# Gated mixing written as one stream over the eight batches, with one of its operations on ScalarE

## The chip, the core and the metric

The kernel runs on one core of a Trainium2 chip. Its engines work side by side, each through its own list of instructions: TensorE (PE in the rows; PEld is its weight load), VectorE (DVE), ScalarE (ACT), GpSimd (POOL) and SyncE (SP), which issues transfers here. They wait for one another at semaphores only. TensorE writes to PSUM, eight banks of 512 f32 values on each of 128 partitions; VectorE and ScalarE read from there. The metric is the device time of one execution in microseconds.

## What is computed

Eight sublayers run one after another on eight batches of 256 tokens with 256 features. Each is `x = layernorm(x + f(x))`. The change touches the fifth, the gated mixing:

```python
x = _layernorm(x + _L1_ffn_ref(...), axis=-1)
x = _layernorm(x + _L2_attn_ref(x, Wu, bu, Wv, bv, Wg1, bg1, Wg2, bg2, conv_w, conv_b), axis=-1)
x = _layernorm(x + _L2_ffn_ref(...), axis=-1)

def _L2_attn_ref(x, Wu, bu, Wv, bv, Wg1, bg1, Wg2, bg2, conv_w, conv_b):
    R, DH = 256, D // 4
    t = conv(x, conv_w)                  # one filter of three taps for each feature, along the tokens
    t_out = t + conv_b
    u = x @ Wu.T + bu
    v = x @ Wv.T + bv
    h = relu(x @ Wg1.T + bg1)            # 64 wide
    gates = sigmoid(h @ Wg2.T + bg2)
    u_gated, v_gated = u * gates, v * gates
    k_cumsum = cumsum(u_gated, axis=1)   # along the tokens
    return t_out + (k_cumsum * v_gated) @ Wu
```

## The kernel before

Everything is f32. The activations stay on the chip from the first sublayer to the last: `x_sb` holds tokens on the partitions, 16 tiles of 128 tokens, and `xT` holds the same with features on the partitions. Ahead of each stage `boundary` finishes the layer norm, turns `x_sb` by TensorE transposes (L161) and copies the result to `xT` (L169); all engines meet at a barrier on both sides of it. The stage of the gated mixing is `l2_mixing`.

For one batch (`T` = 256 tokens) TensorE has two pieces of work. The front is three groups: `g1`, the product of 64 rows (L1618), `u` and `v` (L1623, four products of 256 columns each), and `g2`, the gates (L1628), which needs `hT`, the relu that ScalarE makes of the first product (L1647). The back (L1635, L1637) adds the product of `go` with `Wu` and a product of `tc` with the unit matrix, which turns the convolution, in one PSUM bank.

ScalarE makes the relu and the sigmoid `ga` (L1650). VectorE does the rest of a batch in three pieces. The convolution `tc` is a centre tap with the bias (L1666, one instruction for each half of the features), the tap before (L1669) and the tap after (L1672). The mixing is `ug` and `vg` out of PSUM (L1677, L1678), the cumulative sum `cum` (L1681) and the product `go` (L1683). The output adds the finished bank to `x_sb` (L113) and measures mean and variance for the layer norm (L120, L124, L126).

The order is written by hand, as a hardware loop of four turns of two batches. In a turn TensorE does front, front, back, back. VectorE does convolution and mixing of the first batch, the same of the second, and then both outputs. All eight PSUM banks are in use, two of each kind, one for each batch of a turn: `HY` takes the product of 64 rows first and the stage's output later, `U`, `V`, and `GG` for the gates. So the first product of the next turn waits until VectorE has added the output out of the same bank (semaphore `z_ready`). `mix_ready` counts finished `go`, `y_ps` finished backs, `ga_ready` finished gates.

Of the kernel before, what the change touches and what calls it, by code (L numbers as in the profile page):

```python
# [8 lines left out]
P = 128  # L9
# [34 lines left out]
def ln_scratch(sb, n):  # L44
    return {"stats": sb("ln_stats", [P, n, 6]), "mv": sb("ln_mv", [P, n, 2]), "carrier": sb("ln_carrier", [P, 1])}
# [49 lines left out]
LN_STEPS = 2  # L95
# [1481 lines left out]
def l2_mixing(nc, c, x_sb, mv, xT, w, psum):  # L1577

    R, DH = 256, 64
    with ExitStack() as ctx:  # L1580
        sb = lambda name, shape, dt=F32: ctx.enter_context(nc.sbuf_tensor("l2a_" + name, shape, dt))
        sem = lambda name: ctx.enter_context(nc.semaphore("l2a_" + name))
        hT = sb("hT", [DH, 2, T])
        ga = sb("ga", [P, 2, 2, T])
        ug = sb("ug", [P, 2, 2, T])
        vg = sb("vg", [P, 2, 2, T])
        cum = sb("cum", [P, 2, 2, T])
        go = sb("go", [P, 2, 2, T])
# [8 lines left out]
        h_ready = sem("h_ready")  # L1597
        uv_ps = sem("uv_ps")
        g_ps = sem("g_ps")
        ga_ready = sem("ga_ready")  # L1600
        mix_ready = sem("mix_ready")
        y_ps = sem("y_ps")
        z_ready = sem("z_ready")
        steps = sem("steps")

        with nc.Block() as block:
            @block.tensor
            def _(pe):
                mm = nc.tensor.matmul
                w["early"](pe)  # L1610
                w["late"](pe)
                pe.sem_inc(z_ready, 2)
                with pe.Fori(0, B // 2) as b:
                    for i in range(2):
                        x = lambda k: xT[:, k, bass.ds(b * 2 * T + i * T, T)]
                        pe.wait_ge(z_ready, 2 * b + i + 1)
                        for k in range(KD):
                            last = mm(HY[i][0:DH, 0:T], w["g1"][:, k, :], x(k), start=(k == 0), stop=(k == KD - 1))  # L1618
                        last.then_inc(h_ps, 1)
                        for name, bk in (("u", U), ("v", V)):  # L1620
                            for m in range(2):
                                for k in range(KD):
                                    last = mm(bk[i][:, m * T:(m + 1) * T], w[name][:, k, m * P:(m + 1) * P], x(k),  # L1623
                                              start=(k == 0), stop=(k == KD - 1))
                        last.then_inc(uv_ps, 1)
                        pe.wait_ge(h_ready, 2 * b + i + 1)
                        for m in range(2):
                            last = mm(GG[i][:, m * T:(m + 1) * T], w["g2"][0:DH, m * P:(m + 1) * P], hT[:, i, :], start=True, stop=True)  # L1628
                        last.then_inc(g_ps, 1)
                    for i in range(2):  # L1630
                        pe.wait_ge(mix_ready, 2 * b + i + 1)
                        for t in range(TT):
                            y = HY[i][:, t * D:(t + 1) * D]
                            for k in range(2):
                                mm(y, go[:, i, k, t * P:(t + 1) * P], w["u"][:, k, :], start=(k == 0), stop=False)  # L1635
                            for k in range(KD):
                                last = mm(y[:, k * P:(k + 1) * P], tc[:, i, k, t * P:(t + 1) * P], c["id"], start=False, stop=(k == KD - 1))  # L1637
                        last.then_inc(y_ps, 1)

            @block.scalar  # L1640
            def _(act):
                nc.scalar.preload_act_table(ACT.Sigmoid)
                w["late"](act)
                with act.Fori(0, B // 2) as b:
                    for i in range(2):
                        act.wait_ge(h_ps, 2 * b + i + 1)
                        nc.scalar.activation(hT[:, i, :], HY[i][0:DH, 0:T], ACT.Relu, bias=w["bg1"][0:DH, :]).then_inc(h_ready, 1)  # L1647
                        act.wait_ge(g_ps, 2 * b + i + 1)
                        for m in range(2):
                            last = nc.scalar.activation(ga[:, i, m, :], GG[i][:, m * T:(m + 1) * T], ACT.Sigmoid, bias=w["bg2"][:, m:m + 1])  # L1650
                        last.then_inc(ga_ready, 1)

            @block.vector
            def _(dve):
                st = Steps(dve, steps, L2A_STEPS)
                nc.vector.memset(ones[:, :], 1.0)
                w["early"](dve)
                w["late"](dve)
                with dve.Fori(0, B // 2) as b:
                    st.begin(b)  # L1660
                    for i in range(2):

                        dve.wait_ge(h_ps, 2 * b + i + 1)
                        x = lambda k, at, n: xT[:, k, bass.ds(b * 2 * T + i * T + at, n)]
                        for k in range(KD):
                            last = nc.vector.tensor_scalar(tc[:, i, k, :], x(k, 0, T), w["conv"][:, k, 1:2], w["convb"][:, k:k + 1], ALU.mult, ALU.add)  # L1666
                        st.do(last)
                        for k in range(KD):
                            last = nc.vector.scalar_tensor_tensor(tc[:, i, k, 1:T], x(k, 0, T - 1), w["conv"][:, k, 0:1], tc[:, i, k, 1:T], ALU.mult, ALU.add)  # L1669
                        st.do(last)  # L1670
                        for k in range(KD):
                            last = nc.vector.scalar_tensor_tensor(tc[:, i, k, 0:T - 1], x(k, 1, T - 1), w["conv"][:, k, 2:3], tc[:, i, k, 0:T - 1], ALU.mult, ALU.add)  # L1672
                        st.do(last)
                        dve.wait_ge(uv_ps, 2 * b + i + 1)
                        dve.wait_ge(ga_ready, 2 * b + i + 1)
                        for m in range(2):
                            nc.vector.scalar_tensor_tensor(ug[:, i, m, :], U[i][:, m * T:(m + 1) * T], w["bu"][:, m:m + 1], ga[:, i, m, :], ALU.add, ALU.mult)  # L1677
                            last = nc.vector.scalar_tensor_tensor(vg[:, i, m, :], V[i][:, m * T:(m + 1) * T], w["bv"][:, m:m + 1], ga[:, i, m, :], ALU.add, ALU.mult)  # L1678
                        st.do(last)
                        for m in range(2):  # L1680
                            last = nc.vector.tensor_tensor_scan(cum[:, i, m, :], ones[:, :], ug[:, i, m, :], 0.0, ALU.mult, ALU.add)  # L1681
                        st.do(last)
                        nc.vector.tensor_tensor(go[:, i, :, :], cum[:, i, :, :], vg[:, i, :, :], ALU.mult).then_inc(mix_ready, 1)  # L1683
                    for i in range(2):
                        dve.wait_ge(y_ps, 2 * b + i + 1)
                        add_and_measure(nc, st, x_sb, mv, b * 2 * TT + i * TT, TT, two(HY[i]), lw, z_ready, 2 * b + i + 3)
                    st.end()


L2A_STEPS = 2 * (5 + LN_STEPS)  # L1690

def l2_ffn(nc, c, x_sb, mv, xT, w, psum):
# [1344 lines left out]
```

## Time and profile before

| | |
|---|---|
| time, median of 3 runs | 2721.08 us (2719.87 to 2721.51) |
| profiled execution: its own time, and the span from first to last instruction | 2712.49 us, 2710.7 us |
| TensorE, VectorE and ScalarE busy, share of the span | 87%, 69%, 51% |
| mean granted TensorE clock over the span | 0.943 |
| the gated mixing, first product to last statistics | 1510.25 to 1594.32 us, 84.07 us |
| the next stage, first transposes | 1597.75 us |

A row of the timeline begins with the start in microseconds from the span's start, and the length. The brackets at its end give the idle time of the engine before it and what ended that. An f32 product of the program shows as two records of TensorE, so `x4` is two products of the program. The granted clock is 1.00 at 2.4 GHz and 0.50 at 1.2 GHz, TensorE's two levels.

### The profile page before, as it was taken

Reading aid. Unit: us, or ns where it says so; the run is one execution under the profiler, and the core shown is the slowest. Engines: PE = TensorE matmul, PEld = TensorE weight load, DVE = VectorE, ACT = ScalarE, POOL = GpSimd, SP = SyncE. Lnnn points to the kernel's source line nnn. Section 1 sums busy time; section 2 is a strip of 40 time slices with the busy share of each in tenths; the row PEclk is TensorE's granted clock in tenths of the full one; section 3 lists DMA queues with packets and bytes.
Section 4 is the critical chain, followed back from the end, with each engine's and each line's share of the span. In section 5 each row is a group of like instructions: output and inputs, shape, how many; then the busy total and the mean of one; then the engine's idle time right before and its main releaser. Section 6 shows DMA issues by size and latency. Waiting matters only on the chain. (4 is left out here: it accounts for less than half of the span.)

```text
span 2710.7 us, 41350 instructions
## 1 busy us (share of the span) xinstructions
PE 2367.8 (87%) x13696; PEld 1866.6 (69%) x13696; DVE 1880.1 (69%) x4340; ACT 1373.0 (51%) x3717; POOL 456.8 (17%) x449
## 2 busy tenths in 40 slices
PE   7997999969999999999899779967777865999998
PEld 5665567657777778777777657755555544888887
DVE  3665488966655766575666668957777775888887
ACT  4665488864544544454521123338888773333332
POOL 2442200020000000000000000027777780000000
PEclk9999999989999999999999989979898876999999
DMA  4001077731001100110322000010000004222221
GB/s 150 12 8 67 3 160 147 155 72 36 23 11 35 35 19 15 35 35 18 121 63 63 0 0 0 1 53 9 5 4 4 8 1 159 63 64 72 72 63 59
DMA packets 67406, 130.21 MB, mean 48 GB/s; under 512 B 9944, under 2 KB 23256, under 8 KB 65880
## 3 DMA queue, kind: packets, MB, share of 16 engines
q1 hardware_dynamic: 67296, 128.81, 16.7%
q8 instruction: 61, 1.00, 0.1%
q14 instruction: 49, 0.40, 0.1%
HBM read 119.54 MB, written 2.69 MB: 45 GB/s over the span
## 5 line engine op out<-in xcount | busy, mean ns | idle before, releaser
L2180 POOL TENSOR_TENSOR l3a_pr<-l3a_pr,w_l3a_mask 128x1024 f32<-128x1024 f32 x32 | 75.6, 2361 | 1201.1 <-ACT l3a_pr L2247 1201.1
L2247 ACT ACTIVATE l3a_pr<-psum,l3a_nm 128x128 f32<-128x128 f32 (+1 forms) x512 | 207.4, 430 | 72.9 <-DVE l3a_nm L2355 72.9
L1135 ACT ACTIVATE l1a_pr<-psum,l1a_nb,l1a_rq 128x128 f32<-128x128 f32 (+1 forms) x256 | 127.3, 510 | 77.9 <-DVE l1a_nb L1221 74.1
L2355 DVE TENSOR_REDUCE l3a_nm<-psum 128x2 f32<-128x256 f32 (+1 forms) x256 | 124.8, 550 | 54.7 <-PE psum L2059 54.4
L2647 ACT ACTIVATE l3f_sg<-psum 128x512 f32<-128x512 f32 x96 | 57.5, 599 | 192.5 <-PE psum L2599 192.5
L2597 PE MATMUL psum<-l3f_x_hi,l3f_w_hi 128*128 128x512 f32 x384 | 151.8, 395 | 1.7 <-DVE l3f_w_lo L2683 1.7
L2598 PE MATMUL psum<-l3f_x_lo,l3f_w_hi 128*128 128x512 f32 x384 | 151.5, 395 | 0.0
L2599 PE MATMUL psum<-l3f_x_hi,l3f_w_lo 128*128 128x512 f32 x384 | 150.3, 392 | 0.0
L113 DVE TENSOR_TENSOR x_sb<-psum,x_sb 128x512 f32 (+2 forms) x44 | 36.6, 833 | 142.9 <-PE psum L1074 104.9
L372 POOL TENSOR_TENSOR l0a_pr<-l0a_pr,l0a_rec 128x256 f32<-128x256 f32 (+1 forms) x128 | 101.9, 828 | 142.3 <-DVE l0a_rec L462 142.3
L2631 ACT ACTIVATE l3f_w_hi<-w_l3f_all 128x768 fp32r<-128x768 f32 x96 | 81.4, 849 | 80.8 <-PE psum L2616 79.8
L2267 ACT ACTIVATE l3a_pr<-l3a_pr,l3a_nb,l3a_rec 128x128 f32<-128x128 f32 (+1 forms) x256 | 120.4, 570 | 3.3 <-POOL l3a_nb L2202 3.3
L1037 PE MATMUL psum<-l1a_kT,l1a_qT 128*128 128x128 f32 (+1 forms) x512 | 98.8, 337 | 22.7 <-ACT l1a_pr L1135 15.7
L1074 PE MATMUL psum<-l1a_kT,l1a_ko 128*128 128x256 f32 x512 | 112.6, 381 | 6.1 <-ACT l1a_ko L1124 6.1
L2193 POOL TENSOR_TENSOR l3a_pr<-l3a_pr 128x768 f32<-128x768 f32 x64 | 115.9, 1811 | 5.0
L1074 PEld LDWEIGHTS psum<-l1a_kT,l1a_ko 128*128 128x128 f32 x512 | 96.6, 190 | 20.4 <-issue 7.6
L2614 PE MATMUL psum<-l3f_w_hi,l3f_h_hi 128*128 128x256 f32 x384 | 108.9, 284 | 2.0 <-DVE l3f_h_lo L2733 1.9
L2247 ACT ACTIVATION_READ_ACCUMULATOR l3a_pr<-psum,l3a_nm 128x1 f32 x512 | 110.6, 216 | 0.0
L392 ACT ACTIVATE l0a_pr<-psum,l0a_nm 128x128 f32<-128x128 f32 (+1 forms) x256 | 103.6, 437 | 10.6 <-DVE l0a_nm L449 10.2
L2616 PE MATMUL psum<-l3f_w_hi,l3f_h_lo 128*128 128x256 f32 x384 | 108.7, 283 | 0.0
L2615 PE MATMUL psum<-l3f_w_lo,l3f_h_hi 128*128 128x256 f32 x384 | 108.6, 283 | 0.0
L838 DVE TENSOR_TENSOR l0f_act_h<-l0f_act_h,l0f_cbuf 128x512 f32<-128x512 f32 x128 | 88.2, 689 | 26.8 <-ACT l0f_act_h L728 14.3
(439 smaller groups left out, 6976.4 us busy)
## 6 DMA issues: line engine op xcount, KB each, us to landing
l0f_cbuf<-l0f_c_rows SPq DMA_DIRECT2D x128, 256.0 KB, 4.8
l1a_kT<-l1a_o_dram SPq DMA_DIRECT2D x64, 256.0 KB, 2.8
l3f_cbuf<-l3f_c_rows SPq DMA_DIRECT2D x64, 192.0 KB, 2.8
w_l3f_all<-l3f_all_dram SPq DMA_DIRECT2D x1, 9216.0 KB, 25.6
w_l1f_all<-l1f_c_rows SPq DMA_DIRECT2D x32, 256.0 KB, 3.2
l3f_cbuf<-l3f_c_rows SPq DMA_DIRECT2D x64, 128.0 KB, 2.9
w_l0f_w<-l0f_w_dram SPq DMA_DIRECT2D x2, 2048.0 KB, 10.1
l3f_cbuf<-l3f_c_rows SPq DMA_DIRECT2D x64, 64.0 KB, 2.6
```

The costliest lines, as they stand in the source:

```text
L1074: last = mm(PT[0][:, t * D:(t + 1) * D], oT[:, h, t * P:(t + 1) * P], wo[:, h, :], start=(h == 0), stop=(h == H - 1))
L1135: last = nc.scalar.activation(pr[:, n % 2, i, s], S[n % 2][:, i, s], ACT.Exp, bias=nb[:, n % 2, t, i:i + 1], scale=rq[:, t, 2 * n + i:2 * ...
L2193: nc.gpsimd.tensor_tensor(pr[:, r, 0, heads, :], pr[:, r, 0, heads, :], pr[:, r, 1, heads, :], ALU.add).then_inc(dif_ready, 1)
L2247: last = nc.scalar.activation(pr[:, r, a, g, k], S[:, g, k], ACT.Exp, bias=nm[:, i % 2, g, t:t + 1], accum_out=sums[:, r, a, g, t:t + 1])
L2267: last = nc.scalar.activation(pr[:, r, 1, g, k], pr[:, r, 0, g, k], ACT.Exp, bias=nb2[:, r, g, t:t + 1], scale=rec[:, r, 0, g, t:t + 1])
L2355: last = nc.vector.tensor_reduce(nm[:, i % 2, 2 * pair:2 * pair + 2, t], S[:, 2 * pair:2 * pair + 2, t * P:t * P + (t + 1) * P], AX.X, ALU ...
L2597: mm(bk[n % 2], hi, x_hi[:, k, chunk], start=(k == 0), stop=False)
L2598: mm(bk[n % 2], hi, x_lo[:, k, chunk], start=False, stop=False)
L2599: last = mm(bk[n % 2], lo, x_hi[:, k, chunk], start=False, stop=(k == KD - 1))
L2614: mm(Y[b % 2][:, t, :], h_hi[:, n % 2, tokens], hi, start=False, stop=False)
L2615: mm(Y[b % 2][:, t, :], h_hi[:, n % 2, tokens], lo, start=False, stop=False)
L2616: last = mm(Y[b % 2][:, t, :], h_lo[:, n % 2, tokens], hi, start=False, stop=(e == NH - 1 and t % 2 == 1))
```

## The change

The loop is gone: the eight batches are written out one after another on each engine. The work on TensorE is split into `front(n)` and `back(n)`, and their order is front(0), front(1), back(0), front(2), back(1), and so on to front(7), back(6), back(7). VectorE does convolution and mixing of batch n and then the output of batch n - 1. The product of 64 rows moves from the output's bank to the gates' bank `GG`, where the gates overwrite it after the relu; the output has its two banks to itself. ScalarE makes the centre tap with the bias (`Identity` with a scale and a bias of one value for each partition), ahead of the batch that needs it, and VectorE adds the outer two taps onto that after a wait for the new semaphore `tc_ready`. The semaphore waits follow: the first product waits for the gates of two batches earlier to be read, `u` and `v` for `mix_ready` of two batches earlier, the back for `mix_ready` and for the addition of two batches earlier, the sigmoid for `mix_ready` and the centre tap for `y_ps`, both of two batches earlier.

```diff
-        HY, U, V, GG = [bank(0), bank(1)], [bank(2), bank(3)], [bank(4), bank(5)], [bank(6), bank(7)]
+        Y, U, V, GG = [bank(0), bank(1)], [bank(2), bank(3)], [bank(4), bank(5)], [bank(6), bank(7)]
...
+                def front(n):
+                    i, tokens = n % 2, slice(n * T, (n + 1) * T)
+                    if n >= 2:
+                        pe.wait_ge(ga_ready, n - 1)
+                    for k in range(KD):
+                        last = mm(GG[i][0:DH, 0:T], w["g1"][:, k, :], xT[:, k, tokens], start=(k == 0), stop=(k == KD - 1))
+                    last.then_inc(h_ps, 1)
+                    if n >= 2:
+                        pe.wait_ge(mix_ready, n - 1)
...
+                    pe.wait_ge(h_ready, n + 1)
+                    for m in range(2):
+                        last = mm(GG[i][:, m * T:(m + 1) * T], w["g2"][0:DH, m * P:(m + 1) * P], hT[:, i, :], start=True, stop=True)
+                    last.then_inc(g_ps, 1)
+
+                def back(n):
+                    i = n % 2
+                    pe.wait_ge(mix_ready, n + 1)
+                    if n >= 2:
+                        pe.wait_ge(z_ready, n - 1)
...
-                pe.sem_inc(z_ready, 2)
-                with pe.Fori(0, B // 2) as b:
-                    for i in range(2):
-                        x = lambda k: xT[:, k, bass.ds(b * 2 * T + i * T, T)]
-                        pe.wait_ge(z_ready, 2 * b + i + 1)
...
+                front(0)
+                for n in range(B):
+                    if n + 1 < B:
+                        front(n + 1)
+                    back(n)
...
+                def centre(n):
+                    if n >= 2:
+                        act.wait_ge(y_ps, n - 1)
+                    for k in range(KD):
+                        last = nc.scalar.activation(tc[:, n % 2, k, :], xT[:, k, n * T:(n + 1) * T], ACT.Identity,
+                                                    bias=w["convb"][:, k:k + 1], scale=w["conv"][:, k, 1:2])
+                    last.then_inc(tc_ready, 1)
...
+                centre(0)
+                for n in range(B):
+                    i = n % 2
+                    act.wait_ge(h_ps, n + 1)
...
+                    act.wait_ge(g_ps, n + 1)
+                    if n >= 2:
+                        act.wait_ge(mix_ready, n - 1)
...
+                    if n + 1 < B:
+                        centre(n + 1)
...
+                def convolve(n):
+                    i = n % 2
+                    dve.wait_ge(tc_ready, n + 1)
...
+                for n in range(B):
+                    convolve(n)
+                    mix(n)
+                    if n >= 1:
+                        output(n - 1)
+                output(B - 1)
```

The operations themselves, their shapes and their number stay the same on TensorE. On TensorE, before, in one turn of the loop, this stands from the second batch's `u` on: its front, the back of the first batch, and the back of the second.

```order
L1623 MATMUL psum<-xT,w_l2a_u 128x256 x4
L1623 MATMUL psum<-xT,w_l2a_v 128x256 x4
L1628 MATMUL psum<-l2a_hT,w_l2a_g2 128x256 x2
L1635 MATMUL psum<-w_l2a_u,l2a_go 128x256 x2
L1637 MATMUL psum<-cf_sb,l2a_tc 128x128 x2
L1635 MATMUL psum<-w_l2a_u,l2a_go 128x256 x2
L1637 MATMUL psum<-cf_sb,l2a_tc 128x128 x2
L1635 MATMUL psum<-w_l2a_u,l2a_go 128x256 x2
L1637 MATMUL psum<-cf_sb,l2a_tc 128x128 x2
```

Now, from the `u` of batch 1 on: its front, the back of batch 0, and then the front of batch 2.

```order
L1624 MATMUL psum<-xT,w_l2a_u 128x256 x4
L1624 MATMUL psum<-xT,w_l2a_v 128x256 x4
L1629 MATMUL psum<-l2a_hT,w_l2a_g2 128x256 x2
L1640 MATMUL psum<-w_l2a_u,l2a_go 128x256 x2
L1642 MATMUL psum<-cf_sb,l2a_tc 128x128 x2
L1640 MATMUL psum<-w_l2a_u,l2a_go 128x256 x2
L1642 MATMUL psum<-cf_sb,l2a_tc 128x128 x2
L1617 MATMUL psum<-xT,w_l2a_g1 64x256 x2
L1624 MATMUL psum<-xT,w_l2a_u 128x256 x4
```

A whole front has moved between the back of one batch and the back of the next.

On VectorE, before, at the end of the second batch's mixing in a turn, the output of the first batch follows `go`, and the output of the second follows that:

```order
L1683 TENSOR_TENSOR l2a_go<-l2a_cum,l2a_vg 128x512
L113 ISA
L113 TENSOR_TENSOR x_sb<-psum,x_sb 128x512
L132 REGISTER_ALU
L81 MEMSET l2a_ln_carrier 128x1
L120 BN_STATS l2a_ln_stats<-x_sb 128x6
```

Now, after the `go` of batch 1: the output of batch 0, and at once the outer taps and the mixing of batch 2.

```order
L1708 TENSOR_TENSOR l2a_go<-l2a_cum,l2a_vg 128x512
L113 TENSOR_TENSOR x_sb<-psum,x_sb 128x512
L81 MEMSET l2a_ln_carrier 128x1
L120 BN_STATS l2a_ln_stats<-x_sb 128x6 x2
L81 MEMSET l2a_ln_carrier 128x1
L124 BN_AGGR l2a_ln_mv<-l2a_ln_stats 128x2 x2
L126 COPY mv<-l2a_ln_mv 128x4
L1689 SCALAR_TENSOR_TENSOR l2a_tc<-xT,w_l2a_conv,l2a_tc 128x255 x2
L1693 SCALAR_TENSOR_TENSOR l2a_tc<-xT,w_l2a_conv,l2a_tc 128x255 x2
L1702 SCALAR_TENSOR_TENSOR l2a_ug<-psum,w_l2a_bu,l2a_ga 128x256
```

The second output no longer follows the first; a batch's convolution and mixing lie between them, and the register instructions of the loop are gone.

On ScalarE, now, the stage begins so; before, the relu was the first after the table load, and there was no other activation than the relu and the two of the sigmoid.

```order
L1663 ACT_TABLE_LOAD
L1659 ACTIVATE l2a_tc<-xT,w_l2a_convb,w_l2a_conv 128x256 x2
L1670 ACTIVATE l2a_hT<-psum,w_l2a_bg1 64x256
L1675 ACTIVATE l2a_ga<-psum,w_l2a_bg2 128x256 x2
L1659 ACTIVATE l2a_tc<-xT,w_l2a_convb,w_l2a_conv 128x256 x2
L1670 ACTIVATE l2a_hT<-psum,w_l2a_bg1 64x256
```

The centre taps of the next batch stand ahead of its relu, and one table load serves the stage.

## Rows read from the trace of the kernel before

**Rows 1.** The page: busy time, share of the span, instructions.
```profile
PE 2367.8 (87%) x13696; PEld 1866.6 (69%) x13696; DVE 1880.1 (69%) x4340; ACT 1373.0 (51%) x3717; POOL 456.8 (17%) x449
```
**Rows 2.** Windows, one a turn: length, TensorE busy (records), granted clock, DMA.
```profile
1510.25:1531.43 21.18, 18.63 (x80) 0.92 0.00 0
1531.43:1551.88 20.45, 17.91 (x85) 1.00 0.00 0
...
1572.34:1594.40 22.06, 17.20 (x81) 1.00 0.00 0
```
**Rows 3.** Timeline of TensorE: a back of turn 2, then turn 4.
```profile
1548.29 1.13 PE L1635 MATMUL psum<-w_l2a_u,l2a_go 128*128 128x256 f32 x4 [2.54 <-DVE l2a_go L1683]
...
1551.11 1.08 PE L1618 MATMUL psum<-xT,w_l2a_g 128*64 x4
...
1578.05 1.08 PE L1618 MATMUL psum<-xT,w_l2a_g 128*64 x4
1579.06 1.99 PE L1623 MATMUL psum<-xT,w_l2a_u 128*128 x8
...
1582.71 1.13 PE L1628 MATMUL psum<-l2a_hT,w_l2a_g 64*128 64x256 f32 x4
1583.77 1.13 PE L1635 MATMUL psum<-w_l2a_u,l2a_go 128*128 128x256 f32 x4
...
1589.19 1.13 PE L1635 MATMUL psum<-w_l2a_u,l2a_go 128*128 128x256 f32 x4 [2.54 <-DVE l2a_go L1683]
```
**Rows 4.** Waits in the stage: us in total, times, longest.
```profile
PE psum L1635 <- DVE l2a_go L1683: 10.2, 4, 2.5
...
PEld psum L1623 <- issue: 3.1, 8, 0.4
PEld psum L1628 <- issue: 2.7, 8, 0.3
```
**Rows 5.** Window over the second back of turn 1: length, busy of PE, PEld, DVE, ACT, POOL; clock, DMA.
```profile
1527.10:1531.40 4.30, 4.29 (x16) 3.69 (x16) 1.72 (x8) 0.00 (x0) 0.00 (x0) 0.64 0.00 0
```
**Rows 6.** Timeline of VectorE in turn 4, second batch.
```profile
1582.74 0.73 DVE L1666 TENSOR_SCALAR l2a_tc<-xT,w_l2a_conv,w_l2a_convb 128x256 f32 x2
1583.51 0.88 DVE L1669 SCALAR_TENSOR_TENSOR l2a_tc<-xT,w_l2a_conv,l2a_tc 128x255 f32<-128x255 f32 x2
...
1585.44 0.48 DVE L1677 SCALAR_TENSOR_TENSOR l2a_ug<-psum,w_l2a_bu,l2a_ga 128x256 f32<-128x256 f32 x1
...
1589.06 0.68 DVE L113 TENSOR_TENSOR x_sb<-psum,x_sb 128x512 f32 x1
...
1592.24 0.69 DVE L113 TENSOR_TENSOR x_sb<-psum,x_sb 128x512 f32 x1 [1.10 <-PE psum L1637]
...
1594.15 0.17 DVE L126 COPY mv<-l2a_ln_mv 128x4 f32 x1
```
**Rows 7.** Timeline of turn 4: the table load of the stage, sigmoid, mixing, relu.
```profile
1509.62 1.28 ACT L1642 ACT_TABLE_LOAD   x1 [0.26 <-PEq L149]
...
1578.16 0.84 ACT L1650 ACTIVATE l2a_ga<-psum,w_l2a_bg 128x256 f32<-128x256 f32 x2 [4.23 <-PE psum L1628]
1579.13 0.48 DVE L1677 SCALAR_TENSOR_TENSOR l2a_ug<-psum,w_l2a_bu,l2a_ga 128x256 f32<-128x256 f32 x1 [1.46 <-ACT l2a_ga L1650]
1579.17 0.47 ACT L1647 ACTIVATE l2a_hT<-psum,w_l2a_bg 64x256 f32<-64x256 f32 x1 [0.17 <-PE psum L1618]
```
**Rows 8.** Groups of ScalarE, shapes kept apart, whole span: the nearest activation.
```profile
L2267 ACT ACTIVATE l3a_pr<-l3a_pr,l3a_nb,l3a_rec 128x256 f32<-128x256 f32 x128 | 79.6, 622 | 0.0
```
**Rows 9.** Waits of TensorE over the span: entries to stages, and issue.
```profile
PE psum L1348 <- issue: 2.9, 1, 2.9
...
PE psum L1618 <- PEq L1612: 1.7, 1, 1.7
...
PE psum L255 <- PEq L149: 1.3, 1, 1.3
```
**Rows 10.** Window in the next stage, whose code is written out; columns as in rows 5.
```profile
1640.00:1700.00 60.00, 58.26 (x257) 47.34 (x256) 52.74 (x80) 20.83 (x30) 0.00 (x0) 1.00 0.00 1
```

More of the change, by code:

```diff
@@ L1593, in l2_mixing @@
         two = lambda ap: ap.rearrange("p (k t) -> p k t", k=2)
-        HY, U, V, GG = [bank(0), bank(1)], [bank(2), bank(3)], [bank(4), bank(5)], [bank(6), bank(7)]
+        Y, U, V, GG = [bank(0), bank(1)], [bank(2), bank(3)], [bank(4), bank(5)], [bank(6), bank(7)]
         h_ps = sem("h_ps")
         h_ready = sem("h_ready")
+        tc_ready = sem("tc_ready")
         uv_ps = sem("uv_ps")
@@ L1609, in _ @@
                 mm = nc.tensor.matmul
+                def front(n):
[7 more added lines that the diff above has]
+                        pe.wait_ge(mix_ready, n - 1)
+                    for name, bk in (("u", U), ("v", V)):
+                        for m in range(2):
+                            for k in range(KD):
+                                last = mm(bk[i][:, m * T:(m + 1) * T], w[name][:, k, m * P:(m + 1) * P], xT[:, k, tokens],
+                                          start=(k == 0), stop=(k == KD - 1))
+                    last.then_inc(uv_ps, 1)
+                    pe.wait_ge(h_ready, n + 1)
+                    for m in range(2):
+                        last = mm(GG[i][:, m * T:(m + 1) * T], w["g2"][0:DH, m * P:(m + 1) * P], hT[:, i, :], start=True, stop=True)
+                    last.then_inc(g_ps, 1)
@@ new lines, in back @@
+                def back(n):
[3 more added lines that the diff above has]
+                        pe.wait_ge(z_ready, n - 1)
+                    for t in range(TT):
+                        y = Y[i][:, t * D:(t + 1) * D]
+                        for k in range(2):
+                            mm(y, go[:, i, k, t * P:(t + 1) * P], w["u"][:, k, :], start=(k == 0), stop=False)
+                        for k in range(KD):
+                            last = mm(y[:, k * P:(k + 1) * P], tc[:, i, k, t * P:(t + 1) * P], c["id"], start=False, stop=(k == KD - 1))
+                    last.then_inc(y_ps, 1)
@@ L1610, in _ @@
                 w["early"](pe)
                 w["late"](pe)
-                pe.sem_inc(z_ready, 2)
-                with pe.Fori(0, B // 2) as b:
-                    for i in range(2):
-                        x = lambda k: xT[:, k, bass.ds(b * 2 * T + i * T, T)]
-                        pe.wait_ge(z_ready, 2 * b + i + 1)
[L1617 to L1638, printed above, removed]
@@ L1640, in _ @@
+                front(0)
[3 more added lines that the diff above has]
+                    back(n)
             @block.scalar
             def _(act):
+                def centre(n):
+                    if n >= 2:
+                        act.wait_ge(y_ps, n - 1)
+                    for k in range(KD):
+                        last = nc.scalar.activation(tc[:, n % 2, k, :], xT[:, k, n * T:(n + 1) * T], ACT.Identity,
+                                                    bias=w["convb"][:, k:k + 1], scale=w["conv"][:, k, 1:2])
+                    last.then_inc(tc_ready, 1)
@@ L1642, in _ @@
                 nc.scalar.preload_act_table(ACT.Sigmoid)
+                w["early"](act)
                 w["late"](act)
[L1644 to L1651, printed above, removed]
+                centre(0)
@@ new lines, in _ @@
+                for n in range(B):
+                    i = n % 2
+                    act.wait_ge(h_ps, n + 1)
+                    nc.scalar.activation(hT[:, i, :], GG[i][0:DH, 0:T], ACT.Relu, bias=w["bg1"][0:DH, :]).then_inc(h_ready, 1)
+                    act.wait_ge(g_ps, n + 1)
+                    if n >= 2:
+                        act.wait_ge(mix_ready, n - 1)
+                    for m in range(2):
+                        last = nc.scalar.activation(ga[:, i, m, :], GG[i][:, m * T:(m + 1) * T], ACT.Sigmoid, bias=w["bg2"][:, m:m + 1])
+                    last.then_inc(ga_ready, 1)
+                    if n + 1 < B:
+                        centre(n + 1)
@@ L1653, in _ @@
             @block.vector
             def _(dve):
-                st = Steps(dve, steps, L2A_STEPS)
+                st = Steps(dve, steps, 0)
+                st.begin(0)
+                def convolve(n):
+                    i = n % 2
+                    dve.wait_ge(tc_ready, n + 1)
+                    for k in range(KD):
+                        last = nc.vector.scalar_tensor_tensor(tc[:, i, k, 1:T], xT[:, k, n * T:(n + 1) * T - 1], w["conv"][:, k, 0:1],
+                                                              tc[:, i, k, 1:T], ALU.mult, ALU.add)
+                    st.do(last)
+                    for k in range(KD):
+                        last = nc.vector.scalar_tensor_tensor(tc[:, i, k, 0:T - 1], xT[:, k, n * T + 1:(n + 1) * T], w["conv"][:, k, 2:3],
+                                                              tc[:, i, k, 0:T - 1], ALU.mult, ALU.add)
+                    st.do(last)
@@ new lines, in mix @@
+                def mix(n):
+                    i = n % 2
+                    dve.wait_ge(uv_ps, n + 1)
+                    dve.wait_ge(ga_ready, n + 1)
+                    for m in range(2):
+                        nc.vector.scalar_tensor_tensor(ug[:, i, m, :], U[i][:, m * T:(m + 1) * T], w["bu"][:, m:m + 1], ga[:, i, m, :], ALU.add, ALU.mult)
+                        last = nc.vector.scalar_tensor_tensor(vg[:, i, m, :], V[i][:, m * T:(m + 1) * T], w["bv"][:, m:m + 1], ga[:, i, m, :], ALU.add, ALU.mult)
+                    st.do(last)
+                    for m in range(2):
+                        last = nc.vector.tensor_tensor_scan(cum[:, i, m, :], ones[:, :], ug[:, i, m, :], 0.0, ALU.mult, ALU.add)
+                    st.do(last)
+                    nc.vector.tensor_tensor(go[:, i, :, :], cum[:, i, :, :], vg[:, i, :, :], ALU.mult).then_inc(mix_ready, 1)
@@ L1656, in _, with output @@
+                def output(n):
+                    dve.wait_ge(y_ps, n + 1)
+                    add_and_measure(nc, st, x_sb, mv, n * TT, TT, two(Y[n % 2]), lw, z_ready, n + 1)
                 nc.vector.memset(ones[:, :], 1.0)
@@ L1658, in _ @@
                 w["late"](dve)
[L1659 to L1687, printed above, removed]
@@ L1690 @@
-L2A_STEPS = 2 * (5 + LN_STEPS)
+                for n in range(B):
[4 more added lines that the diff above has]
+                output(B - 1)
 def l2_ffn(nc, c, x_sb, mv, xT, w, psum):
```

## Prediction

> **What bounds the kernel now.** The page first: over the whole span TensorE is busy 87% and VectorE 69% [rows 1]. That is a mean over eight sublayers, and the change touches one, 84.07 us of 2710.7. So the stage is read by itself. The windows over its four turns show no transfer, and TensorE busy for 17 to 19 us of each 20 to 22 [rows 2]. The waits of the stage name what is missing: four times 2.5 us, 10.2 us in all, before the second back of a turn, until VectorE has made `go` [rows 4]. The timeline shows why. In turn 4 TensorE ends the front of the second batch where the first back begins, at 1583.77, and could begin the second back 2.82 us later; it begins at 1589.19 [rows 3]. VectorE meanwhile makes convolution and mixing of the second batch one after the other from 1582.74 to 1589.06 [rows 6]. Nothing else is left for TensorE in that turn, since the next turn's first product needs the bank that VectorE's output has yet to empty. In two turns the wait cost more than itself: the window behind the first one shows a granted clock of 0.64 and a back that takes 4.3 us [rows 5] where turn 2 takes 1551.11 - 1548.29 = 2.82 us [rows 3]; the turns with such a back show 0.92 on the mean [rows 2], and there are two of them (turns 1 and 3).
>
> **Pitches at full clock.** Front: from one `g1` to the next group behind `g2`, 1583.77 - 1578.05 = 5.72 us; back 2.82 us [rows 3]. Eight of each are 8 x (5.72 + 2.82) = 68.3 us. Before, from the first product at 1510.25 [rows 2] to the last addition at 1592.24 [rows 6], it is 82.0 us: 68.3 + 10.2 of waits [rows 4] + twice 4.3 - 2.8 = 1.5 for the slow backs [rows 5], with 0.5 left for hand-over and rounding. So the sum closes.
>
> **The new order, step by step.** From the end of front(n), called 0: sigmoid and hand-over take 1579.13 - (1578.16 - 0.11) = 1.08 us [rows 7]; the mixing is 1589.06 - 1585.44 = 3.62 us [rows 6]; so `go` of batch n lets its back begin at 1.08 + (1589.19 - 1585.44) = 4.83 us. TensorE does back(n - 1) and front(n + 1) in between, 2.82 + 5.72 = 8.54 us. The wait of 2.5 us is covered with 3.7 us to spare, in batches 0 to 6. VectorE needs for a batch the outer taps 1585.44 - 1583.51 = 1.93, the mixing 3.62 and the output 1594.15 + 0.17 - 1592.24 = 2.08 us [rows 6], in all 7.63 us against TensorE's 8.54. It waits 0.9 us a batch and TensorE sets the pace. What is late next is TensorE itself.
>
> **The centre tap.** VectorE loses 0.77 us a batch (1583.51 - 1582.74), 6.2 us in all [rows 6]; with it VectorE's batch would be 8.40 us, just under TensorE's, so it is off the path but widens the margin from 0.1 to 0.9 us. ScalarE gains two activations a batch. The trace has none from SBUF with scale and bias of one value a partition in this stage; the nearest are the sigmoid, 0.84 for two [rows 7], and one of the same shape from SBUF with two such operands, 0.62 each [rows 8]. I take 1.2 us for two, the latter, since it has the same operands. What is queued behind them on ScalarE is the relu, and for the relu TensorE's `g2`. centre(n + 1) starts when back(n - 1) ends; the relu of n + 1 is then done at 0.1 + 1.2 + 0.47 = 1.8 us, and `g2` is due 1582.71 - 1578.05 = 4.66 us after the same moment [rows 3, 7]. Cover: `u` and `v`. Cost nothing. On this the Trainium skill (ScalarE: Activation LUTs, Rules for kernel authors) speaks against the move: it says to do additions and multiplications on VectorE. The rows above have the activation slower than the 0.73 us pair it replaces, but on an engine that idles most of the stage; by rule or row the sum stays, unless VectorE were slow enough to matter.
>
> **The ends.** At the end back(7) has no front to hide behind. front(7) ends at 8 x 5.72 + 6 x 2.82 = 62.7 us from the first product, back(6) at 65.5; back(7) begins at 62.7 + 4.83 = 67.5, a wait of 2.0 us; its bank is added 3.05 us later [rows 3, 6] at 70.5, and the output ends at 72.6. VectorE is free by then: mixing to 67.4, output(6) to 69.5. Before it was 84.07. So **-11.5 us**. At the start the loop's set-up goes: TensorE waited 1.7 us for entry here, 1.3 us at an entry of another stage [rows 9]. That is -0.4, bounds 0 and -0.7. ScalarE's centre(0) runs after the table load [rows 7] and delays the first relu by 1.2 us, under the same cover of 4.66.
>
> **New waits on TensorE.** In six fronts `u` now waits for `mix_ready`, always long given. What a given wait costs is bounded by the gaps in the weight load: 2.7 / 8 = 0.34 us before `g2`, which waits, and 3.1 / 8 = 0.39 us before `u`, which does not wait [rows 4]. So it is between 0 and 6 x 0.34 = 2.0 us; I take 0.4, nearer zero, because `u` has the gap already. Two register instructions per `g1` go, at most a little below nothing. The last back could run at the slow clock after its wait, as in turns 1 and 3: 0 to 1.5 us; in two of four turns a longer wait of 2.5 us left the clock alone, so I take 0.
>
> **Sum.** -11.5 - 0.4 + 0.4 = -11.5 us. The profiled execution, 2712.49 us, becomes 2701.0. It lay 8.6 us below the median of the runs; nothing in this stage explains that, so I take the difference as it is: 2721.1 - 11.5 = **2709.6 us**.
>
> **Rivals.**
> - VectorE sets the pace. If its batch takes over 8.54 us, TensorE waits again. For it: VectorE has three more semaphore hand-overs between pieces. Against: 7.63 us from rows that have these in them. At 9.0 us a batch the saving shrinks by 7 x 0.46 = 3.2 to 8.3 us: 2712.8.
> - ScalarE's queue. The relu stands behind the centre taps, which wait for a back. If two of them take over 4.1 us, `g2` is late each batch; at 5.1 to 5.7 us seven batches lose 7 to 11 us and the time comes back to 2717 to 2721. Against: 0.62 each in the nearest row. A second table for `Identity` would not do it: one load is 1.28 us [rows 7], and the order of the changed kernel shows one for the stage.
> - Slower than before: written-out code arrives late. A fetch that stops TensorE for 2.9 us, as the only issue wait of that kind [rows 9], would have to come more than four times in the stage to eat 11.5 us; at one a batch it is 8 x 2.9 = 23 us and 2733. Against: the next stage is written out too, and TensorE is busy 58.26 of 60 us in it [rows 10]. The Trainium skill (Runtime: NRT & Kernel Launch, Instruction fetch mechanics) says that straight code is fetched ahead in blocks and that crossing one is mostly hidden, while a taken branch can stall. The row agrees for straight code; for the loop here, TensorE shows no such stall at its four turns, so nothing is added to the gain.
>
> **Chances.** 0.80 for the forecast, 0.08 for VectorE's pace, 0.08 for ScalarE's queue, 0.04 for late code. A measurement of this kernel tells 0.2%, 5.4 us, from no change. The first two are faster by more than that: 0.88. The third lies within it: 0.08. The fourth is slower: 0.04. The range: the low end takes the bounds below, -0.7 for the entry, no cost of waits, and two more slow backs in the unprofiled runs of before, 3.0 us, so -15.2: 2705.9. The high end takes 2.0 for the waits, 1.5 for the last back, no gain at the entry, and half the clock loss absent from the runs of before, 1.5 us: -6.5, 2714.6; VectorE's case lies inside. Range 2705.5 to 2715.
>
> **What would show it.** In the profile after: the stage 72 to 73 us long; one wait of TensorE for `go`, about 2 us, before the last back, instead of four; backs and fronts alternating at 8.5 us; granted clock 1.00 through the stage; VectorE waiting about 0.9 us for `ga` in each batch; activations of 0.5 to 0.65 us for the centre tap. Wrong would be: a wait of TensorE for `hT` (ScalarE's queue), a wait for `go` or the output in every batch (VectorE), or gaps with no releaser (code). If the stage shortens as said and the time does not, the later stages gave it back.

## The result and the profile after

| | before | changed |
|---|---|---|
| first comparison, 5 runs each | 2721.08 us (2719.87 to 2724.95) | 2706.93 us (2703.77 to 2708.66) |
| second comparison, on one chip, 25 and 5 runs | 2717.25 us (2712.02 to 2722.68) | 2705.7 us (2702.92 to 2708.13) |
| profiled execution, its own time | 2712.49 us | 2707.9 us |
| the gated mixing, first product to last statistics | 84.07 us | 72.31 us |

The ratio of the first comparison is 0.995 with a 95% interval of 0.9938 to 0.9961, that of the second 0.9959 (0.9946 to 0.9973). The medians differ by 14.2 and 11.6 us. The change is faster by 0.3% to 0.6%.

The waits of TensorE within the stage, and those of VectorE, in the trace of the changed kernel (who waited for whom: us in total, times, longest); they answer to [rows 4]:

```profile
PE psum L1640 <- DVE l2a_go L1708: 1.9, 1, 1.9
PE psum L1617 <- PEq L149: 1.1, 1, 1.1
```

```profile
DVE l2a_ug L1702 <- ACT l2a_ga L1675: 10.5, 8, 2.6
...
DVE l2a_tc L1689 <- ACT l2a_tc L1659: 2.1, 1, 2.1
DVE x_sb L113 <- PE psum L1642: 1.1, 1, 1.1
```

Four waits for `go` have become one. VectorE is the engine that waits now, for the gates, in every batch. A window from the first product to the end of the last back, and one over that back alone (length, busy time of PE, PEld, DVE, ACT, POOL, granted clock, DMA), answer to [rows 2, 5]:

```profile
1584.50:1587.40 2.90, 2.88 (x16) 2.49 (x16) 1.71 (x8) 0.00 (x0) 0.00 (x0) 1.00 0.00 0
1517.10:1587.40 70.30, 68.34 (x320) 52.59 (x320) 54.91 (x145) 19.44 (x41) 0.00 (x0) 1.00 0.00 1
```

TensorE is busy 68.3 of 70.3 us, all of it at the full clock. The timeline of two batches near the end and of the end itself, TensorE's rows first (they answer to [rows 3]), then VectorE's and ScalarE's ([rows 6, 7]):

```profile
1565.43 1.08 PE L1617 MATMUL psum<-xT,w_l2a_g 128*64 128x256 f32 x4
...
1571.14 1.13 PE L1640 MATMUL psum<-w_l2a_u,l2a_go 128*128 128x256 f32 x4
...
1573.96 1.08 PE L1617 MATMUL psum<-xT,w_l2a_g 128*64 128x256 f32 x4
...
1579.67 1.13 PE L1640 MATMUL psum<-w_l2a_u,l2a_go 128*128 128x256 f32 x4
...
1584.50 1.13 PE L1640 MATMUL psum<-w_l2a_u,l2a_go 128*128 128x256 f32 x4 [1.94 <-DVE l2a_go L1708]
```

```profile
1563.69 0.48 DVE L1702 SCALAR_TENSOR_TENSOR l2a_ug<-psum,w_l2a_bu,l2a_ga 128x256 f32<-128x256 f32 x1 [1.26 <-ACT l2a_ga L1675]
...
1565.54 1.09 ACT L1659 ACTIVATE l2a_tc<-xT,w_l2a_convb,w_l2a_conv 128x256 f32<-128x256 f32 x2 [1.97 <-PE psum L1642]
...
1566.54 0.47 ACT L1670 ACTIVATE l2a_hT<-psum,w_l2a_bg 64x256 f32<-64x256 f32 x1
...
1567.31 0.68 DVE L113 TENSOR_TENSOR x_sb<-psum,x_sb 128x512 f32<-128x512 f32 x1
...
1569.18 0.87 DVE L1689 SCALAR_TENSOR_TENSOR l2a_tc<-xT,w_l2a_conv,l2a_tc 128x255 f32<-128x255 f32 x2
...
1572.22 0.48 DVE L1702 SCALAR_TENSOR_TENSOR l2a_ug<-psum,w_l2a_bu,l2a_ga 128x256 f32<-128x256 f32 x1 [1.26 <-ACT l2a_ga L1675]
```

A front takes 1571.14 - 1565.43 = 5.71 us, a back 1573.96 - 1571.14 = 2.82, a batch 8.53. VectorE's own batch, from one mixing to the next without the wait, is 1572.22 - 1563.69 - 1.26 = 7.27 us. The relu is done at 1567.0, 1.6 us after the end of the back, and `g2` begins 4.66 us after that end.

Outside this stage the two profiled executions differ by more than half of what the stage gained. The time from each stage's first transpose to the next, summed over all but the mixing, is 2605.1 us in the first and 2611.5 in the second, though those instructions are the same. The transposes ahead of the first product, which the 84.07 and 72.31 us leave out, took 6.7 us for 5.2 at a granted clock of 0.55 for 0.72; in the twelve traces of this document they take 5.2 to 6.7 us, whatever the kernel. That is why the profiled times differ by 4.6 us only, and why each experiment below is read by its stage in the trace first, and by its time second.

### The profile page after: what moved, and what is told of

Its sections match the earlier page's. It is cut to its first block and busy times, and to the rows that moved or that the text cites. A ratio compares the mean times of both kernels' runs of the same rounds, so it can differ in the third digit from the quotient of the medians.

```text
span 2706.1 us, 41176 instructions
## 1 busy us (share of the span) xinstructions
PE 2373.2 (88%) x13696; PEld 1869.3 (69%) x13696; DVE 1874.4 (69%) x4324; ACT 1381.5 (51%) x3733; POOL 456.8 (17%) x449
## 5 line engine op out<-in xcount | busy, mean ns | idle before, releaser
L392 ACT ACTIVATE l0a_pr<-psum,l0a_nm 128x128 f32<-128x128 f32 (+1 forms) x256 | 103.6, 437 | 11.6 <-DVE l0a_nm L449 11.2
```

## Experiments

### Both kernels once more

The same two programs, on one chip, each with a trace of its own.

> The changed kernel once more, beside the kernel before on the same chip, to size the difference. Theory (TensorE sets the pace of the mixing, all else is as before): the stage, first product to last statistics, is 72.3 us as in its first trace, and the time is 11 to 12 us below the kernel before. Rival (something outside the stage gained too): the time is again 14 us below, with stages other than the mixing shorter by 2 us or more in the sum.

Measured: stage 72.31 us, the same as in the first trace of the changed kernel; 2705.7 us against 2717.25, ratio 0.9959 (0.9946 to 0.9973). The stages other than the mixing sum to 2607.7 us. The theory holds: the difference is 11.6 us, and the other stages are not shorter than in the kernel before (2605.1 and 2608.0 us). So the 2.6 us more of the first comparison are put down to its spread: its five runs of the kernel before have a median 3.8 us above that of these 25, which were made on another occasion. No trace assigns them to a stage.

> The kernel before, once more, with a trace of its own, to see how far two executions of one program differ and in which stages. Theory: the mixing takes 84 us and shows four waits of 2.5 us; one to three of the four backs behind them run at the slow clock, 1.5 us each, so the stage varies from 81 to 87 us; the first stages vary by some us each. Rival (the stage is the same to 0.5 us each time): the variation of the time lies in the other stages alone.

Measured: stage 85.97 us, four waits of 2.54; the ratio against its own program is 1.0004 (0.9993 to 1.0014). The windows over the four backs behind the waits (columns as above; a slow back is one that ran in part at the lower clock level):

```profile
1531.40:1535.80 4.40, 4.36 (x16) 3.76 (x16) 1.75 (x8) 0.00 (x0) 0.00 (x0) 0.62 0.00 0
1552.70:1557.00 4.30, 4.26 (x15) 3.68 (x16) 1.74 (x8) 0.00 (x0) 0.00 (x0) 0.60 0.00 0
1574.08:1578.40 4.32, 4.32 (x22) 3.43 (x23) 2.94 (x12) 0.39 (x1) 0.00 (x0) 1.00 0.00 0
1593.70:1596.70 3.00, 2.96 (x9) 2.56 (x10) 1.75 (x8) 0.00 (x0) 0.00 (x0) 0.54 0.00 0
```

The third window has 1.00 (it reaches into the next front); the other three backs are slow, where two of four were in the first trace [rows 2, 5]. So the stage of one program varies by 1.9 us between two executions, 1.6 of them for one more slow back, and the sum of the others lay at 2608.0 against 2605.1 us: the spread sits in both. The changed kernel's stage was 72.31 us both times; with the waits it lost the variation too.

### The order without the bank, the bank without the order

```diff
                     if n >= 2:
-                        pe.wait_ge(ga_ready, n - 1)
+                        pe.wait_ge(z_ready, n - 1)
                     for k in range(KD):
-                        last = mm(GG[i][0:DH, 0:T], w["g1"][:, k, :], xT[:, k, tokens], start=(k == 0), stop=(k == KD - 1))
+                        last = mm(Y[i][0:DH, 0:T], w["g1"][:, k, :], xT[:, k, tokens], start=(k == 0), stop=(k == KD - 1))
```

> The new order and the centre tap on ScalarE, but the product of 64 rows stays in the output's bank, so that front(n + 1) has to wait until VectorE has added output n - 1, which stands behind the mixing of batch n. Theory (the order pays only with the output's bank to itself): that addition ends 1.08 + 3.62 + 0.69 = 5.4 us after front(n), where back(n - 1) ends after 2.8, so TensorE waits 2.7 us in each of six batches; the stage takes 72.3 + 6 x 2.7 = 88 to 89 us, slower than the loop's 84. Rival (the order alone is what pays, the bank is a detail): 73 to 76 us.

Measured: stage 94.6 us; 2724.09 us, ratio 1.0031 (1.0021 to 1.0041), slower than the kernel before. Its waits for the addition, and two of its batches as windows (busy time and clock):

```profile
PE psum L1617 <- DVE x_sb L113: 15.3, 6, 2.5
```

```profile
1527.60:1540.38 12.78, 10.24 (x40) 7.40 (x40) 7.04 (x20) 2.40 (x5) 0.00 (x0) 0.87 0.00 0
1553.21:1564.36 11.15, 8.61 (x41) 6.59 (x41) 7.05 (x20) 2.40 (x5) 0.00 (x0) 1.00 0.00 0
```

The wait was right (six times 2.5 for 2.7 forecast): 72.3 + 15.3 = 87.6. The other 7 us were not expected. 6.6 of them are the clock: 12.78 against 11.15 us is one batch behind a wait that cost the clock and one that did not, and four of the six waits did (granted clocks of 0.86 to 0.87 over their batches). The order alone makes the kernel slower.

```diff
-                            last = mm(HY[i][0:DH, 0:T], w["g1"][:, k, :], x(k), start=(k == 0), stop=(k == KD - 1))
+                            last = mm(GG[i][0:DH, 0:T], w["g1"][:, k, :], x(k), start=(k == 0), stop=(k == KD - 1))
...
-                        nc.scalar.activation(hT[:, i, :], HY[i][0:DH, 0:T], ACT.Relu, bias=w["bg1"][0:DH, :]).then_inc(h_ready, 1)
+                        nc.scalar.activation(hT[:, i, :], GG[i][0:DH, 0:T], ACT.Relu, bias=w["bg1"][0:DH, :]).then_inc(h_ready, 1)
```

> The loop with its old order; only the product of 64 rows moves to the gates' bank, so the wait for the addition no longer stands ahead of it in fact. Theory (in the old order that wait is long given, since both backs stand before the next front): the stage stays at 84 us, within the 1.5 us of a slow back, with four waits of 2.5 us for go. Rival (the shared bank held the loop up): the four waits shrink and the stage is shorter by 3 us or more.

Measured: stage 84.09 us with four waits of 2.54 and two slow backs; ratio 1.0 (0.999 to 1.0009). The bank alone does nothing. The two edits pay together only: the stage is 94.6 and 84.1 us long with one of them, 72.3 with both.

### The centre tap, in either order

```diff
-                    if n + 1 < B:
-                        centre(n + 1)
...
-                    dve.wait_ge(tc_ready, n + 1)
+                    dve.wait_ge(h_ps, n + 1)
+                    for k in range(KD):
+                        last = nc.vector.tensor_scalar(tc[:, i, k, :], xT[:, k, n * T:(n + 1) * T], w["conv"][:, k, 1:2], w["convb"][:, k:k + 1], ALU.mult, ALU.add)
+                    st.do(last)
```

> The changed kernel with the centre tap back on VectorE. Theory (TensorE sets the pace at 8.54 us a batch, VectorE needs 7.63 + 0.77 = 8.40 with the tap): the stage stays at 72.3 us, 0 to 1 us more, and the 0.9 us that VectorE waits for the gates in each batch shrinks to 0.1. Rival (the tap taken off VectorE is what pays): the stage is longer by up to 8 x 0.77 = 6.2 us, 78 us.

Measured: stage 72.31 us, to the hundredth that of the changed kernel; ratio to before 0.994 (0.9921 to 0.996). VectorE still waits 0.49 us for the gates in each batch of the steady part:

```profile
1568.12 0.48 DVE L1702 SCALAR_TENSOR_TENSOR l2a_ug<-psum,w_l2a_bu,l2a_ga 128x256 f32<-128x256 f32 x1 [0.49 <-ACT l2a_ga L1674]
```

The 0.77 us a batch came out of that wait, 1.26 to 0.49. The centre tap's move has no part in the shorter stage.

```diff
+                        for k in range(KD):
+                            last = nc.scalar.activation(tc[:, i, k, :], xT[:, k, bass.ds(b * 2 * T + i * T, T)], ACT.Identity,
+                                                        bias=w["convb"][:, k:k + 1], scale=w["conv"][:, k, 1:2])
+                        last.then_inc(tc_ready, 1)
...
-                        for k in range(KD):
-                            last = nc.vector.tensor_scalar(tc[:, i, k, :], x(k, 0, T), w["conv"][:, k, 1:2], w["convb"][:, k:k + 1], ALU.mult, ALU.add)
-                        st.do(last)
```

> The loop with its old order and banks; only the centre tap moves to ScalarE. Theory (in the old order convolution and mixing of the second batch stand on the path while TensorE waits): each of the four waits shrinks by 0.77 us, from 2.5 to 1.8, and the stage from 84 to 81 us. Rival (the move saves nothing anywhere, or ScalarE's relu comes late): 84 us or more.

Measured: stage 81.75 us with two slow backs, ratio 0.9979 (0.9965 to 0.9994). The taps stand behind the relu here, ahead of it in the changed kernel. The waits shrank from 2.54 to 1.95 us, by 0.6 for 0.77 expected. The timeline of the second batch of a turn shows what took the rest: VectorE, done earlier, met the gates.

```profile
1569.70 0.48 DVE L1680 SCALAR_TENSOR_TENSOR l2a_ug<-psum,w_l2a_bu,l2a_ga 128x256 f32<-128x256 f32 x1 [0.21 <-ACT l2a_ga L1656]
...
1573.45 1.13 PE L1636 MATMUL psum<-w_l2a_u,l2a_go 128*128 128x256 f32 x4 [1.95 <-DVE l2a_go L1686]
```

So the same move is worth 2.3 us in the stage where VectorE's batch stands on the path, and nothing where it does not.

### The loop written out

The three loops of the stage become Python loops with constant addresses; order, banks and engines stay.

```diff
-                with pe.Fori(0, B // 2) as b:
+                for b in range(B // 2):
```

> The old order, banks and engines, but the four turns written out in place of the loop. Theory (a loop costs TensorE only its entry): entry 0.4 to 0.7 us shorter, the rest the same, stage 84 us within a slow back's 1.5 us. Rival (straight code comes late): gaps without a releaser on TensorE or VectorE, stage longer by 3 us or more. Second rival (the loop's register work and branches cost VectorE time on the path): stage shorter by 1.5 us or more with shorter waits for go.

Measured: stage 83.52 us with two slow backs, against 84.07 with two; ratio 0.9992 (0.998 to 1.0004). The waits for `go` are 2.44 us for 2.54. No gap appears, and little is won: 0.55 us. VectorE's instructions follow one another closer (0.92 us from the tap before to the tap after, for 1.02 in the loop), which is where the shorter waits come from, and its 0.35 to 0.38 us without a releaser at each turn of the loop are gone; those stood ahead of a wait for the gates. In the changed kernel the entry costs 1.1 us for 1.7 in [rows 9], and TensorE has no issue wait in the stage.

### How much room VectorE and ScalarE have

```diff
                     add_and_measure(nc, st, x_sb, mv, n * TT, TT, two(Y[n % 2]), lw, z_ready, n + 1)
+                    for _ in range(2):
+                        st.do(nc.vector.tensor_tensor(junk[:, :, :], xT[:, :, n * T:(n + 1) * T], xT[:, :, n * T:(n + 1) * T], ALU.mult))
```

> The changed kernel with two products of 128x512 added on VectorE after each output (work that nobody uses), 0.69 to 0.8 us each, so VectorE needs 9.0 to 9.2 us a batch. Theory (the pace is the longer of TensorE's 8.54 and VectorE's own sum): the stage grows by 7 x 0.5 to 0.7 = 3.2 to 4.6 us, plus the 1.4 to 1.6 us behind the last output, and TensorE waits for go in the later batches. Rival (VectorE's spare time is larger than 0.9 us): it grows by the 1.4 to 1.6 us of the end alone. Rival (VectorE was on the path already): it grows by 8 x 1.4 = 11 us or more.

Measured: stage to the last statistics 75.41 us, 3.1 more, and the added pair of 1.4 behind it; ratio 0.9951 (0.9934 to 0.9968). The size fell short of the 3.2 to 4.6, and the way there was another. TensorE waited for `go` once, not in the later batches:

```profile
1567.01 1.41 DVE L1715 TENSOR_TENSOR l2a_junk<-xT 128x512 f32<-128x512 f32 x2
1570.28 0.48 DVE L1703 SCALAR_TENSOR_TENSOR l2a_ug<-psum,w_l2a_bu,l2a_ga 128x256 f32<-128x256 f32 x1
...
1579.04 0.48 DVE L1703 SCALAR_TENSOR_TENSOR l2a_ug<-psum,w_l2a_bu,l2a_ga 128x256 f32<-128x256 f32 x1
...
1582.79 1.42 PE L1641 MATMUL psum<-w_l2a_u,l2a_go 128*128 128x256 f32 x4 [3.31 <-DVE l2a_go L1709]
```

```profile
1582.80:1587.40 4.60, 4.54 (x16) 3.76 (x16) 2.98 (x10) 0.00 (x0) 0.00 (x0) 0.63 0.00 0
```

VectorE's batch is 1579.04 - 1570.28 = 8.76 us, not 9.0 to 9.2. TensorE stayed at 8.53 a batch, since `go` has 3.7 us to spare there, while VectorE fell behind by 0.23 a batch, 1.4 us over the six batches to the last. The last back has no front ahead of it to cover this, so the whole lag shows there, as a wait of 3.31 for 1.94. Behind it the last back ran at a granted clock of 0.63 and took 4.6 us for 2.9. The lag of 1.4 and the clock's 1.7 are the 3.1 measured. That this is close to the 3.2 expected is chance: by the rule of the expectation 0.23 us a batch is worth 7 x 0.23 = 1.6 us, and the clock is not in it.

```diff
                     last.then_inc(tc_ready, 1)
+                    if n >= 1:
+                        for j in range(4):
+                            for k in range(KD):
+                                nc.scalar.activation(junk[:, j, k, :], xT[:, k, n * T:(n + 1) * T], ACT.Identity,
+                                                     bias=w["convb"][:, k:k + 1], scale=w["conv"][:, k, 1:2])
```

> The changed kernel with four further pairs of centre taps on ScalarE behind the real pair of batches 1 to 7 (into a tile that nobody reads), so that the relu stands behind five pairs. A pair took 1.09 us; ten activations that overlap take 5.1 us. Theory (the relu has 4.66 us from the end of a back, of which the real pair and the relu use 1.7): the relu is now done 5.7 us after the back, g2 is 1.0 to 1.2 us late in six fronts and about 1.9 in front(1), and the stage grows by 8 to 9 us to 80 to 82. Rival (the relu is not on a path that matters): the stage stays at 72.3 us. Rival (each added microsecond on ScalarE counts): it grows by 7 x 4 = 28 us.

Measured: stage 80.9 us, 8.6 more for 8 to 9; ratio 0.9973 (0.9962 to 0.9984). TensorE's waits name the relu:

```profile
PE psum L1630 <- ACT l2a_hT L1676: 6.4, 7, 1.5
```

The window over the back behind the longest of them:

```profile
1527.90:1532.20 4.30, 4.30 (x16) 3.69 (x16) 3.11 (x7) 0.84 (x2) 0.00 (x0) 0.60 0.00 0
```

The total was met, its parts were not. The waits are 1.53 us in front(1) and 0.81 to 0.82 in six fronts, for 1.9 and 1.0 to 1.2 expected; with the 0.07 us that each adds around it they make 6.9 us. The other 1.7 are one slow back, behind the wait of 1.53, which the expectation did not have. The relu's queue is a real path with nearly the room that the prediction gave it: ten taps took 4.93 us, so the relu was done 0.11 + 4.93 + 0.45 = 5.49 us after the back, 0.83 behind the 4.66. About 3 us of further work are free, and what lies beyond reaches TensorE. At 1.09 us for the pair the changed kernel is far from it.

### A shorter end

`g2` stands between `u` and `v`. In the last batch the unit-matrix products come first and the mixing goes half by half:

```diff
+                    if n == B - 1:
+                        pe.wait_ge(z_ready, n - 1)
+                        pe.wait_ge(steps, 6 * n)
...
+                                mm(y[:, k * P:(k + 1) * P], tc[:, i, k, t * P:(t + 1) * P], c["id"], start=(t == 0 and k == 0), stop=False)
+                        for k in range(2):
+                            pe.wait_ge(mix_ready, n + 1 + k)
+                            for t in range(TT):
+                                last = mm(Y[i][:, t * D:(t + 1) * D], go[:, i, k, t * P:(t + 1) * P], w["u"][:, k, :], start=False, stop=(k == 1 and t == TT - 1))
```

> The changed kernel with its end shortened. The gates' product g2 stands between u and v in every front, so the sigmoid is done before v is. In the last batch the unit-matrix products of the back are made before go is awaited, and the mixing is done half by half, so that only two products are left behind the second half of go. Theory (TensorE's pace stays 8.54 us a batch; only the end waits): the mixing of the last batch begins 0.85 us earlier, the back has 1.8 us less behind go, one more hand-over on VectorE costs 0.2: stage 69.9 us (69.5 to 70.4), and the time lies 2.4 us below the changed kernel, too little to tell in the runs. Rival (the earlier g2 makes TensorE wait for the relu): the pace grows by some tenths a batch and the stage is 72 us or more.

Measured: stage 70.94 us, 1.4 less for 2.4 expected; 2700.1 us, ratio to before 0.9937 (0.9924 to 0.9951). The interval overlaps with the changed kernel's, so only the trace tells the two apart. About half of the missing 1.0 us lies with TensorE and half with VectorE:

```profile
1580.00 1.97 PE L1645 MATMUL psum<-w_l2a_u,l2a_go 128*128 128x256 f32 x8
...
1580.70 0.68 DVE L113 TENSOR_TENSOR x_sb<-psum,x_sb 128x512 f32<-128x512 f32 x1
...
1582.57 0.68 DVE L113 TENSOR_TENSOR x_sb<-psum,x_sb 128x512 f32<-128x512 f32 x1
```

The last back is done at 1581.97, 68.4 us after the first product, where it was 70.3 in the changed kernel: 1.9 us earlier for 2.4 expected. More was not to be had, because TensorE has no wait left in the stage and its work alone is 68.3 us; the expected 69.9 us left no room for that and an output of 2.0 us. The mixing began 0.5 us earlier, not 0.85. Then VectorE is still in output(6), which it began when the mixing was done, and adds output(7) 0.6 us after the back without a wait. From the start of the last mixing at 1576.74 to the end at 1584.54 it has no gap. The end is VectorE's by that 0.6 us, and TensorE's own work stands right behind it.

## Why the prediction was right, and where it was off

- **The bound.** Right. TensorE's 68.3 us at full clock is what the stage consists of; after the change it is busy 68.3 of 70.3.
- **The pitches** of 5.72 and 2.82 us, read off one turn, came back as 5.71 and 2.82 (5.69 in the first front).
- **The wait of 2.5 us is covered.** Right: it is gone in batches 0 to 6. The last one was to be 2.0 us and is 1.94.
- **The ends.** 72.6 us forecast, 72.31 measured. Entry: -0.4 taken, 1.1 for 1.7 us measured, so -0.5, which falls ahead of the first product.
- **New waits on TensorE.** 0.4 taken, bounds 0 and 2.0; they cost nothing. The front is 5.71 us with the added wait before `u` and was 5.72 without.
- **Slow clock in the last back.** 0 taken of 0 to 1.5. It did not come here, nor in the repetition. It came behind the 3.31 us wait of the variant with added products on VectorE.
- **VectorE's batch** was mis-sized: 7.63 us by the rows, 7.27 measured, so it waits 1.26 and not 0.9 us. The output takes 1569.18 - 1567.31 = 1.87 us to the start of the next instruction (1.96 to its own end) for 2.08, and the outer taps take about 1.8 for 1.93; the mixing is 3.62 as before. The rows came from the loop, where register instructions stand between the parts. The loop written out, with the old order, has the shorter output too, 1.97 us, and the shorter taps, so writing out is what shortens them. It made the margin larger and changed nothing.
- **The centre tap.** "Off the path" was right, shown by the run without it: 72.31 us both ways. Its size, 1.2 us for two, was 1.09. The advice of the Trainium skill (ScalarE: Activation LUTs, Rules for kernel authors) to keep additions and multiplications on VectorE is borne out in price, 1.09 us against 0.73, and is of no weight in this order.
- **The rivals.** VectorE's pace as a rival had an error in its mechanism: I charged every microsecond of excess in the batch where it arises. The run with added products shows that TensorE does not notice it in batches 0 to 6, where `go` has 3.7 us to spare, and that the lag of all of them is owed at the last back, in full: 6 x 0.23 = 1.4 us. So the size, 7 times the excess, was nearly right and the place was not, and a slow back can come on top. ScalarE's queue was priced rightly: by the threshold of 4.1 us for two taps, 4.93 us make `g2` 0.83 us late, and the waits were 0.81 to 0.82. The total of 80.9 us does not show this, since 1.7 of it are the clock. Late code did not appear. On that the Trainium skill (Runtime: NRT & Kernel Launch, Instruction fetch mechanics) agrees with the two written-out variants, where TensorE has no issue wait. The stall that the Trainium skill gives there for a taken branch to code that is not fetched yet is not to be seen on TensorE in this loop: writing it out saved 0.55 us in four turns, 0.4 of it in the waits for VectorE.
- **The time.** -11.5 us forecast; 14.2 in the first comparison and 11.6 in the second, whose interval for the ratio, in microseconds, is 7 to 15. The size holds in the stage (84.07 - 72.31 = 11.8 us). What stays open is how much the slow backs add to it on the mean, since one more slow back in the kernel before is 1.5 to 1.7 us and a trace shows one execution, and where the 2.6 us between the two comparisons come from. The range had no term for the other stages, whose sum moves by up to 8 us from one execution to the next. The changed kernel's medians, 2706.9 and 2705.7 us, lie near its low end of 2705.5 although the stage came out as forecast; that they fell inside is in part luck.

## What to carry to other kernels

Where an engine waits at the same place in every turn, ask what other batch's work it could do there, and then which buffer forbids it: here order and bank take 12 us off the stage together, and apart the order adds 10.5 us, the clock's part included, and the bank gives nothing. Before taking work off an engine, check that it is on the path in the order that you end with; the same move was worth 2.3 us in the old order and 0.00 in the new. An engine that is a little slower than the pace shows no wait while the pipeline has slack, but its lag adds up and is owed where nothing covers it: here 0.23 us a batch came back as 1.4 us at the last back. And when a total agrees with the forecast, add up its waits all the same: twice here a slow back made up for parts that were too large.

## What was not expected of the hardware

- Waits of 2.5 us on TensorE cost the clock more often than not. Over the four traces in the old order with waits of 2.44 to 2.55 us (the kernel before twice, the own bank, the loop written out), 9 of 16 such waits were followed by products at the lower level, and 4 of 6 in the variant with the shared bank; of the nine waits of 1.94 or 1.95 us two were. The one wait of 3.31 us and the one of 1.53 us were too, the six of 0.8 us behind that were not. Each time costs 1.5 to 1.7 us, more than half of a wait of 2.5 us. In the shared-bank variant this made 6.6 us that the sum of the waits had not shown. What decides between two waits of the same length stays open.
- The time of one program, outside the changed stage, moved by up to 8 us between executions (2604.0 to 2612.0 us over the twelve traces), while the changed stage was 72.31 us in both traces of the changed kernel and in that with the centre tap on VectorE.
